# Weight comparisons spread over the last two batches with four staging slots, and the first masks made ahead of the second gates

## The chip, the cores and the metric

One Trainium2 chip, one core of it. The metric is the device time of one launch in microseconds (us). Engine names are those of the profile: PE is the matrix engine, DVE the vector engine, ACT the scalar engine, POOL the GpSimd engine, SP the engine whose queue issues most of the transfers. PEld is the weight load of PE. The kernel is written with one instruction stream for each engine and explicit semaphores, so each engine works strictly through its own list.

## The reference

One transformer-like layer on x of 16 x 256 x 256 in fp32, with a context of the same shape. First an mLSTM attention with 8 heads of 32, then a feed-forward network with ternary weights:

```
x = x + mlstm(layernorm(x), ctx, ctx, gates)      # gates: 16 columns, tanh cap, log-sigmoid, cumulative sum and max
z = layernorm(x)
h = silu(z @ w1.T * s1) * (z @ w2.T * s2)          # 256 -> 1024
h = gelu(h @ h1.T * s3)                            # 1024 -> 1024
h = gelu(h @ h2.T * s4)                            # 1024 -> 1024
x = x + h @ w3.T * s_w3                            # 1024 -> 256
```

The decay matrix of the attention is exp(log_d - row maximum) below the diagonal, multiplied on the scores of each head.

## The kernel before, in words

The 16 sequences are worked in 8 pairs (`PAIRS`), each 512 tokens wide. All weights of the feed-forward network stay in SBUF as `wgt`, 22 units (`UNITS`) of 128 x 1024 fp32, loaded once in a rounding format (fp32r). Activations are split into a high and a low part (`h_hi`, `h_lo`) in that format, and every product is done twice, once for each part, so that the result is as good as fp32 as long as the weights are exactly representable. That is tested at run time: each weight unit is loaded a second time without rounding (`load_raw`, 512 KB) and compared on DVE with the resident one (`compare`, L868). The marks of difference are counted (`inexact`), summed over columns (`decide`, L874), summed over partitions by a matmul on PE (`count_inexact`, L1176), and turned into an integer `general` (L876). At its end every engine reads `general` and branches (`if_general`): if any weight was changed by rounding, the whole feed-forward network is done again by a slow exact path. With the ternary weights of this input it never is.

The main loop runs over i = 0..7. `batch(i)` on each engine does the feed-forward network of pair i and, woven into it by hand, the attention of pair i+1 (`a_stage`) and the gates of pair i+2 (`g_stage`). So iteration 6 has no gates any more, and iteration 7 has neither. On PE an iteration is: `swiglu` (64 matmuls of 512 columns, L1105 and L1106), `hidden` for two layers (2 x 128 matmuls of 512 columns, L1129 and L1130; for the first two of the eight output tiles the sum runs as the inputs come in, and from the third on everything must be there), `project` (64 matmuls of 256 columns, L1162 and L1163). ACT makes silu or gelu and `h_hi`, DVE makes `h_lo` (L840, L844), and PE needs both.

The comparisons stand in iteration 7 on DVE: after each `lo(i, 0, m)` of the first hidden layer two of them (0 to 15), after the first three `lo(i, 1, m)` of the second another two each (16 to 21), then `decide`. The raw units go through two slots, placed in `decay`, the tile of the decay matrices, with bf16 marks beside each slot. `load_raw(n)` is issued by SP when comparison n-2 is done. SP starts these loads in iteration 7, after the store of pair 6.

Before the loop stands a prologue, which does the attention of pair 0 and the gates of pairs 0 and 1 with nothing beside them, in this order. On PE: `turn_z(0)`, `gates(0)`, some clock-keeping matmuls, `turn_z(1)`, `turn_rows(0)` (L1032, which gives the columns `cols` for the masks), `gates(1)` (L1017 with the keys and the high part, L1024 with z, which needs the low part of z from POOL, L435), `scores(0, 0)` and `scores(0, 1)` (L1050), `make_state(0)` (L1059), values and state. On DVE: scans of pair 0 (L706, L718), normalization of z of pair 1, `gain_b` (L947), `add_gate_low(1)` (L699, waits for `gates(1)`), `masks(0)` (L735, 32 operations with two SBUF inputs, `decay` and `future`, and a column of `cols`), `floors(0)` (L743), `weigh_scores(0, 0)` and `(0, 1)` (L751, four operations each, one input from PSUM). On ACT the exponentials of the masks (`decays`, L531) and the high parts, on POOL the low parts (L431, L435) and `weigh_keys` (L426). `scores(0, 1)` waits for all of `weigh_scores(0, 0)`, since both use the same PSUM banks, and `make_state(0)` for all of `weigh_scores(0, 1)`.

Of the kernel before, what the change touches and what calls it, by code (L numbers as in the profile page):

```python
# [12 lines left out]
BF16 = mybir.dt.bfloat16  # L13
# [8 lines left out]
KH = HID // P  # L22
# [9 lines left out]
PAIRS = BATCH // W  # L32
# [14 lines left out]
LAYERS = 4  # L47
GELU = 4
STAGE = 4

ROW_G, ROW_FLOOR, ROW_CHUNK = 0, 32, 64
ROWS = ROW_CHUNK + BH
# [1 line left out]
ROW_LOW = 64  # L54
SPLIT_COLS = ROW_LOW + GATE_COLS
SPLIT_WIDTH = SPLIT_COLS + HEADS

RSQRT_STEPS = 11
NORM_STEPS = 3 + RSQRT_STEPS
# [9 lines left out]
def build(nc, x, ctx_tok, ctx_t, gate_w, gate_b, outnorm_w, w_cols, scales, w3_s, out):  # L69
    with ExitStack() as stack:  # L70
# [3 lines left out]
        def sem(name):  # L74
            return stack.enter_context(nc.semaphore(name))
# [70 lines left out]
        s_raw = [sem(f"s_raw{n}") for n in range(2)]  # L146
# [134 lines left out]
        block = stack.enter_context(nc.Block())  # L281

        def raw(n):
            return decay[:, n % 2 * 3 * UNIT // 2:n % 2 * 3 * UNIT // 2 + UNIT]

        def marks(n):
            return decay[:, n % 2 * 3 * UNIT // 2 + UNIT:(n % 2 + 1) * 3 * UNIT // 2].bitcast(BF16)

        @block.sync
        def _(sp):  # L290
# [43 lines left out]
                sp.dma_start(out[i], xs[i % 2][:]).then_inc(s_out, 16)  # L334

            def load_raw(n):
                if n < 2:
                    sp.wait_ge(s_mix, MIX_STEPS * PAIRS)
                else:
                    sp.wait_ge(s_inexact, n - 1)  # L340
                sp.dma_start(raw(n), w_cols[:, n * UNIT:(n + 1) * UNIT]).then_inc(s_raw[n % 2], 16)

            load_z(0)
            sp.dma_start(gw_in, gate_w).then_inc(s_gw, 16)
# [17 lines left out]
            for i in range(PAIRS):  # L362
                j, g = i + 1, i + 2
                if j < PAIRS and j > 1:
                    load_x(j)
                if g < PAIRS:
                    load_z(g)
                    load_ctxT(g)
                    load_v(g)
                if j < PAIRS:  # L370
                    keep_x1(j)
                if g < PAIRS:
                    keep_rows(g)
                    spread_max(g)
                if i == PAIRS - 1:
                    for n in range(UNITS):
                        load_raw(n)
                store(i)
            sp.wait_ge(s_x1kept, 16 * PAIRS)
# [97 lines left out]
        def _(act):  # L477
# [120 lines left out]
            take_gate_low(0)  # L598
            soft_cap(0)
            softplus(0)  # L600
            split_keys(1)
            take_zT(1)
            take_gate_low(1)
            take_cols(0)
            soft_cap(1)
            decay_cols(0)
            decays(0)
            softplus(1)
            take_near(0)
            take_cols(1)  # L610
# [12 lines left out]
        def _(dve):  # L623
# [247 lines left out]
            def decide():  # L871

                dve.wait_ge(s_inexact, UNITS)
                dve.tensor_reduce(inexact_sum[:], inexact[:], AX.X, ALU.add).then_inc(s_inexact_sum, 1)  # L874
                dve.wait_ge(s_inexact_all, 1)
                dve.tensor_scalar(general[:], ps_a[0:1, 0, 0:1], 0.0, None, ALU.is_gt).then_inc(s_general, 1)  # L876

            def batch(i, a_stage, g_stage, last=False):
                j, g = i + 1, i + 2
                for m in range(KH):  # L880
                    swiglu(i, m)
                    if m >= 1:
                        lo_1(i, m - 1)
                lo_1(i, KH - 1)
                if a_stage:
                    masks(j)
                    floors(j)
                    weigh_scores(j, 0)
                for m in range(KH):
                    lo(i, 0, m)  # L890
                    if a_stage and m == 1:
                        weigh_scores(j, 1)
                    if g_stage and m == 3:
                        norm_1_stats(g)
                    if g_stage and m == 4:
                        norm_rsqrt(s_norm1, g)
                        norm_1_apply(g)
                    if a_stage and m == 5:
                        take_state(j)
                    if a_stage and m == 6:  # L900
                        take_far(j)
                    if a_stage and m == 7:
                        take_num(j)
                        mix_divide(j)
                    if last:
                        compare(2 * m)
                        compare(2 * m + 1)
                if a_stage:
                    mix_square(j)
                    mix_rsqrt(j)  # L910
                    residual(j)
                    norm_2_stats(j, xs[j % 2])
                for m in range(KH):
                    lo(i, 1, m)
                    if a_stage and m == 1:
                        norm_rsqrt(s_norm2, j)
                        norm_2_apply(j, xs[j % 2])
                    if g_stage and m == 2:
                        add_gate_low(g)
# [4 lines left out]
                    if last and m < 3:  # L924
                        compare(2 * KH + 2 * m)
                        compare(2 * KH + 2 * m + 1)
                    if last and m == 3:
                        decide()
                if a_stage:
                    take_z2T(j)  # L930
                finish(i)

            dve.memset(rows[:], 0.0).then_inc(s_cleared, 1)
            norm_1_stats(0)
# [13 lines left out]
            add_gate_low(1)  # L948
            dve.wait_ge(s_ident, 8)
            masks(0)  # L950
            floors(0)
            weigh_scores(0, 0)
            weigh_scores(0, 1)
            take_state(0)
            scan_f(1)
# [27 lines left out]
        def _(pe):  # L983
# [194 lines left out]
            def batch(i, a_stage, g_stage, as_is=False, last=False):  # L1178
                j, g = i + 1, i + 2
                if as_is:  # L1180
                    pe.wait_ge(s_y, W * i)
                weights_in(pe, 0)
                pe.wait_ge(s_z2lo, i + 1)
                for m in range(KH):
                    swiglu(i, m, as_is)
                    if a_stage and m == 4:
                        scores(j, 0)

                def after_2(m):
                    if a_stage and m == 3:  # L1190
                        scores(j, 1)
                    if a_stage and m == 5:
                        make_state(j)
                        values(j, 0, 0)
                    if a_stage and m == 6:
                        read_state(j)

                def after_3(m):
                    if g_stage and m == 2:
                        gates(g)  # L1200
                    if a_stage and m == 6:
                        turn_z2(j)
                    if g_stage and m == 7:
                        turn_rows(g)
                    if last and m == 5:
                        count_inexact()
# [24 lines left out]
                project(i, as_is)  # L1231

            def keep_clock(products):

# [6 lines left out]
            gates(0)  # L1241
            keep_clock(12)
            pe.wait_ge(s_cleared, 1)
            turn_z(1)
            turn_rows(0)
            gates(1)
            scores(0, 0)
            scores(0, 1)
            make_state(0)
            for b in range(W):  # L1250
# [65 lines left out]
```

## Time and profile before

| | us |
|---|---|
| median of 3 runs | 873.95 |
| lowest, highest | 872.20, 879.17 |
| profiled execution, its own time | 878.02 |
| its span, first to last instruction | 876.3 |
| mean granted TensorE clock | 0.944 of full speed |
| PE busy (matmul) | 811.6 (93%) |
| DVE busy | 564.1 (64%) |
| ACT busy | 380.3 (43%) |
| POOL busy | 62.8 (7%) |

The profiled execution took 1.7 us more than its span, and 4.1 us more than the median of the runs. A busy share of 93% on PE is an average over a prologue of about 100 us, seven iterations and a last one, and says nothing about any one of them.

### The profile page before, as it was taken

What the parts mean: (1) busy time and instruction counts of PE and PEld (TensorE: products, weight loads), DVE (VectorE), ACT (ScalarE), POOL (GpSimd) and SP (SyncE); (2) the same over time, 40 slices, a digit from 0 to 9 for tenths busy, and PEclk for the clock granted to TensorE, in tenths of its full rate; (3) what the DMA queues carried; (4) which work ended last, traced back from release to release, by engine and by line L of the source; (5) the groups of instructions that cost most, each with busy time, mean ns of one, the idle gap of its engine ahead of it and who ended that gap; (6) DMA issues with size and microseconds to landing.
All of it is one profiled execution on the core that took longest, in us unless ns stands there. A gap on an engine that the chain in (4) does not pass through costs nothing.

```text
span 876.3 us, 11793 instructions
## 1 busy us (share of the span) xinstructions
PE 811.6 (93%) x4610; PEld 692.5 (79%) x4610; DVE 564.1 (64%) x1336; ACT 380.3 (43%) x551; POOL 62.8 (7%) x54
## 2 busy tenths in 40 slices
PE   5448699999999999999999999999999999999586
PEld 5348588887888888888888888888888788888466
DVE  4474586857857585958776695758585765564551
ACT  2230363455535472355535462556345553443131
POOL 4240000200020000100020001000020000000000
PEclk7556799999999999999999999999999999999788
DMA  7573200122000400131003200040012100024650
GB/s 248 212 283 119 117 1 25 50 97 73 25 26 31 162 25 5 46 124 46 25 25 120 74 25 26 25 169 1 25 50 98 49 1 1 25 73 140 179 161 26
DMA packets 14635, 66.40 MB, mean 76 GB/s; under 512 B 2032, under 2 KB 2416, under 8 KB 11504
## 3 DMA queue, kind: packets, MB, share of 16 engines
q1 hardware_dynamic: 13280, 54.07, 17.7%
q0 software_dynamic: 1296, 11.53, 3.5%
q8 instruction: 38, 0.62, 0.3%
q14 instruction: 21, 0.17, 0.1%
HBM read 57.08 MB, written 8.52 MB: 75 GB/s over the span
## 4 chain that ended last, share of the span: by engine, by line
PE 73%; DVE 16%; DMA 5%; issue 3%; ACT 2%; POOL 1%; DVEq 0%; POOLq 0%; ACTq 0%
PE ps_f L1129 19%; PE ps_f L1130 18%; DVE decay L735 8%; PE ps_a L1068 7%; PE ps_f L1105 7%; PE ps_f L1106 7%; DMA decay<-w_cols 5%; PE ps_f L1162 4%; PE ps_f L1163 4%; DVE decay L751 2%; PE ps_a L1050 2%; PE ps_a L987 2%; DVE decay L868 2%; PE ps_a L1059 1%; PE ps_a L1078 1%
## 5 line engine op out<-in xcount | busy, mean ns | idle before, releaser
L1129 PE MATMUL ps_f<-h_hi,wgt 128*128 128x512 f32 x1024 | 407.5, 398 | 9.2 <-DVE h_lo L844 9.2
L1130 PE MATMUL ps_f<-h_lo,wgt 128*128 128x512 f32 x1024 | 401.9, 392 | 0.0
L1129 PEld LDWEIGHTS ps_f<-h_hi,wgt 128*128 128x128 f32 x1024 | 194.0, 189 | 51.5 <-DVE h_lo L844 10.7
L1130 PEld LDWEIGHTS ps_f<-h_lo,wgt 128*128 128x128 f32 x1024 | 194.1, 190 | 38.5
L844 DVE TENSOR_TENSOR h_lo<-work,h_hi 128x512 fp32r<-128x512 f32 x128 | 86.1, 688 | 125.4 <-ACT h_hi L563 124.3
L558 ACT ACTIVATE work<-ps_f,scl 128x512 f32<-128x512 f32 x128 | 87.4, 683 | 179.9 <-PE ps_f L1130 179.8
L1105 PE MATMUL ps_f<-h_hi,wgt 128*128 128x512 f32 x256 | 101.4, 396 | 0.0
L1106 PE MATMUL ps_f<-h_lo,wgt 128*128 128x512 f32 x256 | 100.3, 392 | 0.0
L545 ACT ACTIVATE work<-ps_f,scl 128x512 f32<-128x512 f32 x64 | 44.1, 689 | 92.6 <-PE ps_f L1106 92.6
L563 ACT ACTIVATE h_hi<-work 128x512 fp32r<-128x512 f32 x128 | 80.9, 632 | 4.1
L835 DVE SCALAR_TENSOR_TENSOR work<-ps_f,scl,work 128x512 f32<-128x512 f32 x64 | 48.1, 751 | 49.2 <-ACT work L545 49.2
L735 DVE SCALAR_TENSOR_TENSOR decay<-decay,cols,future 128x128 f32<-128x128 f32 x256 | 73.0, 362 | 0.0
L1068 PEld LDWEIGHTS ps_a<-v_aug,decay 128*128 128x128 f32 x512 | 67.7, 209 | 1.6
L1068 PE MATMUL ps_a<-v_aug,decay 128*128 128x33 f32 x512 | 66.0, 287 | 0.0
L1162 PE MATMUL ps_f<-wgt,h_hi 128*128 128x256 f32 x256 | 62.2, 285 | 0.0
L1163 PE MATMUL ps_f<-wgt,h_lo 128*128 128x256 f32 x256 | 61.8, 283 | 0.0
L1105 PEld LDWEIGHTS ps_f<-h_hi,wgt 128*128 128x128 f32 x256 | 48.0, 188 | 14.9 <-DVE work L835 4.0
L1106 PEld LDWEIGHTS ps_f<-h_lo,wgt 128*128 128x128 f32 x256 | 48.1, 188 | 8.7
L531 ACT ACTIVATE decay<-decay 128x1024 f32<-128x1024 f32 x32 | 33.9, 1060 | 38.7 <-DVE decay L735 38.7
L1163 PEld LDWEIGHTS ps_f<-wgt,h_lo 128*128 128x128 f32 x256 | 49.1, 192 | 0.1
L1162 PEld LDWEIGHTS ps_f<-wgt,h_hi 128*128 128x128 f32 x256 | 49.1, 192 | 0.1
L426 POOL TENSOR_TENSOR num<-v_aug,e_cols 128x256 f32<-128x256 f32 x16 | 17.3, 1099 | 377.7 <-ACT e_cols L524 377.7
(148 smaller groups left out, 785.7 us busy)
## 6 DMA issues: line engine op xcount, KB each, us to landing
decay<-m_rows SPq DMA_DIRECT2D x16, 1024.0 KB, 5.9
decay<-w_cols SPq DMA_DIRECT2D x22, 512.0 KB, 4.2
wgt<-w_cols POOLq DMA_DIRECT2D x5, 1024.0 KB, 9.5
v_aug<-ctx_tok SPq DMA_DIRECT2D x8, 528.0 KB, 3.7
z<-x SPq DMA_DIRECT2D x8, 512.0 KB, 4.4
xs<-x SPq DMA_DIRECT2D x8, 512.0 KB, 3.6
wgt<-w_cols POOLq DMA_DIRECT2D x2, 2048.0 KB, 9.8
x_kept<-xs SPq DMA_DIRECT2D x8, 512.0 KB, 2.6
```

The costliest lines, as they stand in the source:

```text
L558: act.activation(work[:, m % GELU], ps_f[:, (turn_of(i) + m) % 4], ACT.Gelu, scale=scl[:, 2 + layer, m:m + 1]).then_inc(s_gelu, 1)
L563: act.activation(h_hi[1 - layer][:, m], work[:, m % GELU], ACT.Copy).then_inc(s_hi, 1)
L735: last = dve.scalar_tensor_tensor(part, part, cols[:, t, row:row + 1], future[:], ALU.subtract, ALU.add)
L835: dve.scalar_tensor_tensor(work[:, 2 + m % 2], ps_f[:, bank], scl[:, 1, m:m + 1], work[:, m % 2], ALU.mult, ALU.mult).then_inc(s_hf, 1)
L844: dve.tensor_tensor(h_lo[1 - layer][:, m], work[:, m % GELU], h_hi[1 - layer][:, m].bitcast(F32), ALU.subtract).then_inc(s_lo, 1)
L1068: last = pe.matmul(ps_a[:, 2 + b, h * DV:(h + 1) * DV], decay_of(b, h, t), v_aug[:, b * TILES + t, h, :], start=True, stop=True)
L1105: pe.matmul(ps_f[:, bank + half], w, moving(z2_hi[:, c], as_is), start=(c == 0), stop=False)
L1106: last = pe.matmul(ps_f[:, bank + half], w, moving(z2_lo[:, c], as_is), start=False, stop=(c == CH - 1))
L1129: pe.matmul(ps_f[:, bank], w, moving(h_hi[layer][:, k], as_is), start=(k == 0), stop=False)
L1130: last = pe.matmul(ps_f[:, bank], w, moving(h_lo[layer][:, k], as_is), start=False, stop=(k == KH - 1))
L1162: pe.matmul(to, moving(h_hi[0][:, k, q * P:(q + 1) * P], as_is), w, start=(k == 0), stop=False)
L1163: last = pe.matmul(to, moving(h_lo[0][:, k, q * P:(q + 1) * P], as_is), w, start=False, stop=(k == KH - 1))
```

## The change

Two parts. (1) The comparisons are spread over iterations 6 and 7. The raw units get four slots of their own, which fill `decay`; the marks move to `z`, which nothing reads after pair 7 is normalized. Comparisons 0 to 5 stand in iteration 6, one after each `lo(6, 1, m)` for m = 2 to 7; 6 to 13 in the first and 14 to 21 in the second hidden layer of iteration 7, one after each `lo`. SP issues loads 0 to 9 in iteration 6, before the store of pair 6, and the others after it. The sum over columns is taken before `finish(7)`, the matmul of the count stands after the last `project`, and `general` is made after `finish(7)`. (2) In the prologue PE turns the rows of pair 0 before z of pair 1, and does `scores(0, 0)` before `gates(1)`. ACT takes the columns of pair 0 before the keys of pair 1, and its exponentials stand ahead of the low gates of pair 1. DVE makes the masks, the floors and the first weighted scores of pair 0 before `add_gate_low(1)`.

```
 def raw(n):
-    return decay[:, n % 2 * 3 * UNIT // 2:n % 2 * 3 * UNIT // 2 + UNIT]
+    return decay[:, n % RAW * UNIT:(n % RAW + 1) * UNIT]          # RAW = 4
 def marks(n):
-    return decay[:, ... ].bitcast(BF16)
+    return z[:].rearrange("p q d -> p (q d)")[:, n % 2 * UNIT // 2:(n % 2 + 1) * UNIT // 2].bitcast(BF16)

 SP  load_raw(n)
-    if n < 2:   sp.wait_ge(s_mix, MIX_STEPS * PAIRS)
-    else:       sp.wait_ge(s_inexact, n - 1)
+    if n < RAW: sp.wait_ge(s_mix, MIX_STEPS * PAIRS)
+    else:       sp.wait_ge(s_inexact, n - RAW + 1)
 SP  loop over i, after keep_x1, keep_rows, spread_max
+    if i == PAIRS - 2:
+        for n in range(COMPARED_BEFORE_LAST + RAW): load_raw(n)    # COMPARED_BEFORE_LAST = 6
     if i == PAIRS - 1:
-        for n in range(UNITS): load_raw(n)
+        for n in range(COMPARED_BEFORE_LAST + RAW, UNITS): load_raw(n)

 DVE compare(n)
-    dve.wait_ge(s_raw[n % 2], 16 * (n // 2) + 16)
+    dve.wait_ge(s_raw[n % RAW], 16 * (n // RAW) + 16)
+    if n >= 2:
+        dve.wait_ge(s_inexact, n - 1)
 DVE batch, first hidden layer, after lo(i, 0, m)
     if last:
-        compare(2 * m); compare(2 * m + 1)
+        compare(COMPARED_BEFORE_LAST + m)
 DVE batch, second hidden layer, after lo(i, 1, m)
-    if last and m < 3: compare(2 * KH + 2 * m); compare(2 * KH + 2 * m + 1)
-    if last and m == 3: decide()
+    if last: compare(COMPARED_BEFORE_LAST + KH + m)
+    elif a_stage and not g_stage and m >= KH - COMPARED_BEFORE_LAST:
+        compare(m - KH + COMPARED_BEFORE_LAST)
 DVE batch, end
+    if last: sum_inexact()          # the reduction that stood in decide()
     if a_stage: take_z2T(j)
     finish(i)
+    if last: decide()               # waits for the count, makes general
 PE  batch
-    if last and m == 5: count_inexact()      # in the second hidden layer
     project(i, as_is)
+    if last: count_inexact()

 ACT prologue                 DVE prologue                   PE prologue
  softplus(0)                  gain_b += 1                    wait s_cleared
 +take_cols(0)                -add_gate_low(1)               +turn_rows(0)
 +decay_cols(0)                wait s_ident                   turn_z(1)
  split_keys(1)                masks(0)                      -turn_rows(0)
  take_zT(1)                   floors(0)                     +scores(0, 0)
 +decays(0)                    weigh_scores(0, 0)             gates(1)
  take_gate_low(1)            +add_gate_low(1)               -scores(0, 0)
 -take_cols(0)                 weigh_scores(0, 1)             scores(0, 1)
  soft_cap(1)
 -decay_cols(0)
 -decays(0)
  softplus(1)
```

## Rows read from the trace of the kernel before

**Rows 1.** The page, granted TensorE clock in tenths, 40 equal slices.

```profile
PEclk7556799999999999999999999999999999999788
```

**Rows 2.** Waits of PE, 756 to 876.3 us: total, times, longest.

```profile
PE ps_f L1129 <- DVE h_lo L844: 9.2, 3, 4.3
PE ps_a L1176 <- DVE inexact_sum L874: 3.3, 1, 3.3
```

**Rows 3.** Chain that ended last, 725 us to the end: start, length, what.

```profile
...
794.04 1.24 DVE decay L868 x2
795.30 3.73 DMA decay<-w_cols
...
```

**Rows 4.** Timeline of PE, 756 us to the end: start, length, instruction.

```profile
...
762.60 0.28 PE L1162 MATMUL ps_f<-wgt,h_hi 128*128 128x256 f32 x1
...
770.27 0.40 PE L1105 MATMUL ps_f<-h_hi,wgt 128*128 128x512 f32 x1
...
785.00 0.39 PE L1129 MATMUL ps_f<-h_hi,wgt 128*128 128x512 f32 x1
...
794.12 0.39 PE L1129 MATMUL ps_f<-h_hi,wgt 128*128 128x512 f32 x1
...
869.11 0.28 PE L1163 MATMUL ps_f<-wgt,h_lo 128*128 128x256 f32 x1
```

**Rows 5.** Two-microsecond stretch: busy of PE, PEld, DVE, ACT, POOL; clock; DMA.

```profile
826.00:828.00 2.00, 1.82 (x4) 0.90 (x4) 1.23 (x2) 0.00 (x0) 0.00 (x0) 0.50 0.82 242
```

**Rows 6.** Timeline of DVE and SP in iterations 6 and 7.

```profile
745.05 0.34 SPq L330 DMA_DIRECT2D x_kept<-xs  x1
...
751.91 1.90 DVE L844 TENSOR_TENSOR h_lo<-work,h_hi 128x512 fp32r<-128x512 f32 x3
...
765.10 1.22 DVE L826 TENSOR_TENSOR h_lo<-ps_a,h_hi 128x1024 fp32r<-128x1024 f32 x1 [0.22 <-ACT h_hi L540]
...
794.04 1.22 DVE L868 SCALAR_TENSOR_TENSOR decay<-decay,wgt 128x1024 bf16<-128x1024 f32 x1
```

**Rows 7.** All transfers into `decay` by SP, from issue to landing.

```profile
DMA to landing us min/median/max: 3.4/4.6/7.4
```

**Rows 8.** Timeline of SP, the last instruction of the list.

```profile
871.34 0.34 SPq L334 DMA_DIRECT2D out<-xs  x1
```

**Rows 9.** Timeline of the prologue and the start of iteration 0.

```profile
25.28 2.33 POOL L431 TENSOR_TENSOR h_lo<-ctxT,h_hi 128x1024 fp32r<-128x1024 f32 x1 [5.74 <-ACT h_hi L484]
25.45 2.71 DVE L718 TENSOR_TENSOR_SCAN state<-rows 16x256 f32<-16x256 f32 x1
...
34.79 0.29 DVE L947 TENSOR_SCALAR gain_b<-gain_b 128x256 f32<-128x256 f32 x1
...
38.90 2.35 POOL L435 TENSOR_TENSOR h_lo<-zT,h_hi 128x1024 fp32r<-128x1024 f32 x1 [11.28 <-ACT h_hi L493]
...
44.20 8.49 DVE L735 SCALAR_TENSOR_TENSOR decay<-decay,cols,future 128x128 f32<-128x128 f32 x32
...
46.24 7.51 POOL L426 TENSOR_TENSOR num<-v_aug,e_cols 128x256 f32<-128x256 f32 x2 [3.95 <-ACT e_cols L524]
...
53.19 2.47 DVE L751 SCALAR_TENSOR_TENSOR decay<-ps_a,decay 128x512 f32<-128x512 f32 x4
...
55.71 2.09 PE L1050 MATMUL ps_a<-work 32*128 32x128 f32 x32 [9.38 <-DVE decay L751]
...
60.50 2.10 PE L1059 MATMUL ps_a<-v_aug,num 128*128 128x132 f32 x8 [2.70 <-DVE decay L751]
...
64.41 0.68 DVE L718 TENSOR_TENSOR_SCAN xs<-rows 16x256 f32<-16x256 f32 x1
...
118.63 9.21 DVE L735 SCALAR_TENSOR_TENSOR decay<-decay,cols,future 128x128 f32<-128x128 f32 x32
...
119.73 1.39 POOL L426 TENSOR_TENSOR num<-v_aug,e_cols 128x256 f32<-128x256 f32 x2 [64.38 <-ACT e_cols L524]
```

**Rows 10.** Chain that ended last, 20 to 60 us.

```profile
41.30 2.06 PE ps_f L1024 x8
```

More of the change, by code:

```diff
@@ L49 @@
 STAGE = 4
+RAW = 4
 ROW_G, ROW_FLOOR, ROW_CHUNK = 0, 32, 64
@@ L56 @@
 SPLIT_WIDTH = SPLIT_COLS + HEADS
+COMPARED_BEFORE_LAST = 6
 RSQRT_STEPS = 11
@@ L145, in build @@
         s_wgt = [sem(f"s_wgt{n}") for n in range(LAYERS)]
-        s_raw = [sem(f"s_raw{n}") for n in range(2)]
+        s_raw = [sem(f"s_raw{n}") for n in range(RAW)]
         s_inexact = sem("s_inexact")
@@ L283, in raw @@
         def raw(n):
-            return decay[:, n % 2 * 3 * UNIT // 2:n % 2 * 3 * UNIT // 2 + UNIT]
+            return decay[:, n % RAW * UNIT:(n % RAW + 1) * UNIT]
         def marks(n):
-            return decay[:, n % 2 * 3 * UNIT // 2 + UNIT:(n % 2 + 1) * 3 * UNIT // 2].bitcast(BF16)
+            return z[:].rearrange("p q d -> p (q d)")[:, n % 2 * UNIT // 2:(n % 2 + 1) * UNIT // 2].bitcast(BF16)
         @block.sync
@@ L336, in load_raw @@
             def load_raw(n):
-                if n < 2:
+                if n < RAW:
                     sp.wait_ge(s_mix, MIX_STEPS * PAIRS)
                 else:
-                    sp.wait_ge(s_inexact, n - 1)
-                sp.dma_start(raw(n), w_cols[:, n * UNIT:(n + 1) * UNIT]).then_inc(s_raw[n % 2], 16)
+                    sp.wait_ge(s_inexact, n - RAW + 1)
+                sp.dma_start(raw(n), w_cols[:, n * UNIT:(n + 1) * UNIT]).then_inc(s_raw[n % RAW], 16)
             load_z(0)
@@ L374, in _ @@
                     spread_max(g)
+                if i == PAIRS - 2:
+                    for n in range(COMPARED_BEFORE_LAST + RAW):
+                        load_raw(n)
                 if i == PAIRS - 1:
-                    for n in range(UNITS):
+                    for n in range(COMPARED_BEFORE_LAST + RAW, UNITS):
                         load_raw(n)
@@ L600, in _ @@
             softplus(0)
+            take_cols(0)
+            decay_cols(0)
             split_keys(1)
             take_zT(1)
+            decays(0)
             take_gate_low(1)
-            take_cols(0)
             soft_cap(1)
-            decay_cols(0)
-            decays(0)
             softplus(1)
@@ L866, in compare, with sum_inexact, decide @@
                         weights_in(dve, layer)
-                dve.wait_ge(s_raw[n % 2], 16 * (n // 2) + 16)
+                dve.wait_ge(s_raw[n % RAW], 16 * (n // RAW) + 16)
+                if n >= 2:
+                    dve.wait_ge(s_inexact, n - 1)
                 dve.scalar_tensor_tensor(marks(n), raw(n), 1.0, wgt[:, n * UNIT:(n + 1) * UNIT].bitcast(F32),
                                          ALU.mult, ALU.not_equal, accum_out=inexact[:, n:n + 1]).then_inc(s_inexact, 1)
-            def decide():
+            def sum_inexact():
                 dve.wait_ge(s_inexact, UNITS)
                 dve.tensor_reduce(inexact_sum[:], inexact[:], AX.X, ALU.add).then_inc(s_inexact_sum, 1)
+            def decide():
                 dve.wait_ge(s_inexact_all, 1)
@@ L905, in batch @@
                     if last:
-                        compare(2 * m)
-                        compare(2 * m + 1)
+                        compare(COMPARED_BEFORE_LAST + m)
                 if a_stage:
@@ L923, in batch @@
                         scan_m(g)
[L924 to L928, printed above, removed]
+                    if last:
+                        compare(COMPARED_BEFORE_LAST + KH + m)
+                    elif a_stage and not g_stage and m >= KH - COMPARED_BEFORE_LAST:
+                        compare(m - KH + COMPARED_BEFORE_LAST)
+                if last:
+                    sum_inexact()
                 if a_stage:
@@ L931, in batch @@
                 finish(i)
+                if last:
+                    decide()
             dve.memset(rows[:], 0.0).then_inc(s_cleared, 1)
@@ L947, in _ @@
             dve.tensor_scalar(gain_b[:], gain_b[:], 1.0, None, ALU.add).then_inc(s_gain, 1)
-            add_gate_low(1)
             dve.wait_ge(s_ident, 8)
@@ L952, in _ @@
             weigh_scores(0, 0)
+            add_gate_low(1)
             weigh_scores(0, 1)
@@ L1204, in after_3 @@
                         turn_rows(g)
-                    if last and m == 5:
-                        count_inexact()
                 def within_2(m):
@@ L1231, in batch @@
                 project(i, as_is)
+                if last:
+                    count_inexact()
             def keep_clock(products):
@@ L1243, in _ @@
             pe.wait_ge(s_cleared, 1)
+            turn_rows(0)
             turn_z(1)
-            turn_rows(0)
+            scores(0, 0)
             gates(1)
-            scores(0, 0)
             scores(0, 1)
```

## The prediction

> **What bounds the kernel now.** I read the granted clock first [rows 1]. It is full for most of the run and low at both ends, in the prologue and again in the last three slices, from about 810 us. A low clock at the end means that PE had been standing still. The waits of PE in that stretch [rows 2] name who: three waits for a low part from DVE, 9.2 us, and one for the sum of the marks, 3.3 us. They are 12.5 us in all, and between the start of iteration 7 and those waits there is no other. The chain of work that ended last [rows 3] says what DVE was doing: two comparisons, then a load of raw weights, and that pattern repeats 11 times. With two slots and two comparisons in a row DVE always catches up with the loads, and `lo` stands behind them in its queue. So iteration 7 is bound by the loads. Iterations 0 to 6 are bound by PE, which has no gap there. The prologue is bound by a chain over several engines, with PE mostly waiting.
>
> **Part 1, the last iteration: what PE would need.** All terms are from one timeline [rows 4]. `swiglu` runs from 770.27 to 785.00, 14.73 us. The hidden layers run at one matmul in 0.228 us where nothing waits: 40 matmuls lie between the starts at 785.00 and 794.12. 256 of them are 58.4 us. `project` of iteration 6 lasts from 762.60 to 770.27, 7.67 us. Sum: 80.8 us, so the last product would end at 851.0. Before, the last one starts at 869.11 and ends about 0.12 later, at 869.2. The difference is 18.2 us, of which 12.5 are the waits [rows 2]; the other 5.7 are products at half clock after each wait [rows 5], 0.43 instead of 0.23 us each, and refilling.
>
> Does the new placing hold those 18.2? In iteration 7 one comparison of 1.22 us [rows 6] follows each `lo` of 0.69. PE needs one output tile of 16 matmuls, 3.65 us, for each `lo`, so DVE has 1.7 us to spare each time. Only the first two tiles of a layer come as a pair, and nothing is needed of them before the next layer. The last `lo` of a layer is the tight one: PE asks for it after 28 matmuls of the next layer, 6.4 us on (in `project` after 28 of 0.12, 3.4 us). It takes 0.7 (gelu), 0.6 (high part) and 0.7 us, and the comparison before it ended long ago. No wait there.
>
> The loads: a slot is free after its comparison and needed again four comparisons later, 4 x 3.65 - 1.2 = 13.4 us. Loads into `decay` took 3.4 to 7.4 us [rows 7]. The margin is 6 us at the worst measured landing. Only at the start, with four in flight after the copy of x1, are they slower than a pair was, bounded below by 3.4 and above by four times the median, 18 us. I take about 10 us for the fourth, nearest to two in flight at 3.7 us of bare waiting [rows 3].
>
> **Iteration 6.** SP issues the first four right after the copy of x1 at 745.05 [rows 6], so from about 745.4 to 746.8. The first comparison stands after the third `lo`. Before, three `lo` ran together at 751.91, because DVE was busy with the normalization until then, so comparison 0 starts at about 752.6, 7 us after its load was issued. Six comparisons, 7.3 us, now go between 752.6 and the last `lo` at about 764.2; DVE was idle for over 9 us of that stretch. The last comparison moves `take_z2T(7)` from 765.10 [rows 6] to about 766.1, done at 767.4, and PE asks for it at 770.27 [rows 4]. What is queued behind a late load here: `lo(6, 1, m)`, then that, then `finish(6)`, whose bank PE wants again in `swiglu`. The cover is about 3 us, and costs one for one beyond it. SP holds the store of pair 6 behind loads 0 to 9; the last of these waits for comparison 5 at about 766, and the store was due at 772. The marks in `z` cost nothing, and neither does the added wait on comparison n-2, which is older work of the same engine. Cost of iteration 6: 0, up to 2.
>
> **The end.** The count's matmul stands after the last product, and `general` after `finish(7)`, so all engines take their branch about 2 us after the last product and no earlier. The store, issued at 871.34 with the span's end 5.0 us later [rows 8], covers it: SP must wait for its landing anyway. I take 0.2 us; bounds 0 and 2, since no row shows a branch by itself. Part 1: -18.2 + 0.2 = -18.0 us.
>
> **Part 2, the prologue.** Before, the masks start at 44.20, after `gates(1)` and `add_gate_low(1)` [rows 9]. What they need is there earlier: DVE is free after L947, at 35.08, the rows have been scanned since 29 us and their broadcast was issued at 29.6, so landed by 37.0 at the latest by its 7.4 [rows 7]; turning the rows and taking the columns is 1 us and fits before. So the masks start at 35.1 (or up to 37), last 8.5, and with the floors the first weighted scores start at 44.3 in place of 53.19: 8.9 us less. After that the order is as before: 2.5 us of weighing, `scores(0, 1)` 2.1 us, weighing again, then `make_state(0)` at 51.6 in place of 60.50. On ACT the exponentials (1.06 us each) come after the high part of z at about 38.8, when two masks are finished or nearly so; they keep up. On PE `scores(0, 0)`, 2.1 us, now stands before `gates(1)`, but the second half of `gates(1)` waits until POOL is done at 41.25 anyway.
>
> That half waits for POOL's low part of z, 38.90 to 41.25 [rows 9], and now this subtraction meets the masks, which it did not before. Three places in rows 9 show what such a meeting costs. A scan of 0.68 us (at 64.41) took 2.71 when POOL's L431 ran (at 25.45): DVE was held for the whole of POOL's operation. The first weighing of keys, which takes 1.39 at 119.73, took 7.51 at 46.24, until the masks ended: POOL was held. And at 118.63 the masks took 9.21 instead of 8.49: both shared. If DVE is held, the masks grow by 2.35 and the gain is 8.9 - 2.35 = 6.6. If POOL is held until the masks end at 43.6, its subtraction ends at about 46, the second half of `gates(1)` (2.06 [rows 10]) at 48.1 and `scores(0, 1)` behind it in PE's queue starts at 48.1 in place of 46.9: gain 7.7. `add_gate_low(1)` in DVE's queue then waits until about 48.9, still before `scores(0, 1)` is done. If nothing is held, 8.9. I take 7.2, between the first two, since all three rows show a price.
>
> The Trainium skill (GPSIMD Engine Reference, section 8, Key points) says that GpSimd shares its SBUF interfaces with VectorE and contends with instructions that have two SBUF inputs. The masks have two, the weighing has one, so by that rule the meeting costs in the masks alone; the three rows agree that it costs, and only they say how much. Without that rule the sum would be 1.7 us lower.
>
> The moved L431 is neutral: it held the scan at 25.45 for 2.0 us, and after the change it falls on the small steps of the normalization of pair 1 instead, which are held as long. L947 ends where it did, within 0.5 us.
>
> Everything behind `make_state(0)` is relative to it: the values at half clock, the clock-keeping products, the mixing. The clock may change its levels at another point of that sequence. In slices 3 and 4 [rows 1] it stays near half while PE does the small products of the attention, so I expect no rise there; the phase is worth 1.5 us either way.
>
> **Sum.** 878.02 (the profiled execution's own time) - 18.0 - 7.2 = 852.8. The median of the runs is 4.1 lower. If those 4.1 lie in the stretch bound by loads, they go with it, and all runs come to about 852.8; if they lie elsewhere, the median comes to 848.7. The loads are what varies most in this trace (3.4 to 7.4 us for the same kind), so I lean to the first: 851.5.
>
> **Rivals.**
> - The tail keeps a part. If four loads in flight land late or DVE's queue makes PE wait in spite of my slack, some waits of [rows 2] stay, each with its stretch at half clock; half of 18.2 is 9.1, so about 861. For it: six new comparisons in the busiest stretch of DVE. Against: 13.4 us for a load of at most 7.4. Chance 0.08.
> - The prologue gives nothing. Something between 60 and 100 us may be set by the clock or by a transfer, not by `make_state(0)`, or both holdings above add up. 878.02 - 18.0 = 860, or 857 with half the gain. Against: the chain runs through L1059 and on without a transfer. Chance 0.09.
> - More than the sum: no holding at all, and the clock rises during the denser products at 35 to 43 us and stays for part of the attention. 845. Chance 0.06.
> - Slower: the loads are slower than the comparisons ask. If a load took 20 us with four in flight, a round of four comparisons would take 21.3 us in place of 14.6, and the 5.5 rounds cost 37 us: 890. It eats the whole gain from about 18 us a load, and starts to cost at 13.4. The slowest of all in the trace is 7.4 [rows 7]. Chance 0.02.
> - It doesn't do what it says: the waits of PE simply move from one iteration to the other, near 872. Against: iteration 6 has over 9 us of idle DVE. Chance 0.02.
>
> **How the numbers follow.** The forecast has 0.73. A measurement of this kernel can tell about 1%, 8.7 us, from no change; everything under 865.2 is faster by that. Forecast, partial tail, empty prologue and the better case lie there: 0.96. Same: 0.02. Slower: 0.02. The range goes from the better case, 845, to the empty prologue, 860, and leaves out less than 2 in 10.
>
> **What would show it.** In the new profile: no wait of L1129 for L844 from iteration 6 on, clock 1.0 to the end, six L868 between about 735 and 760 and 16 later, none of them right behind another but at the start of a layer; last product about 81 us after the first L1105 of iteration 7; `make_state` (L1059's line) at 51 to 54 us; a POOL subtraction longer than 2.35 us or masks longer than 8.5. It is wrong if PE waits at the start of the last `project` or `swiglu`, if comparisons in iteration 6 show idle time for a load longer than 3 us, or if the span's end lies more than 6 us behind the last store.

## The result, and the profile after

Median 851.49 us (850.59 to 853.00) against 874.37; ratio 0.9727, 95% interval 0.9699 to 0.9755 (the two medians alone give 0.9738). The profiled execution took 851.26, its span is 849.5: 26.8 us less than before in one pair of profiles.

The page of the changed kernel, its granted clock and the chain that ended last by engine (PE was 73% and the transfers 5% of it before):

```profile
PEclk7756899999999999999999999999999999999999
PE 80%; DVE 16%; ACT 2%; issue 2%; DMA 0%; POOL 0%; DVEq 0%; ACTq 0%
```

The low digits at the end [rows 1] are gone; those of the prologue are still there. The busy time in iteration 7, by one stretch (busy of PE, PEld, DVE, ACT, POOL; clock; DMA share; GB/s):

```profile
761.00:842.00 81.00, 81.00 (x391) 67.81 (x389) 42.85 (x69) 32.01 (x49) 0.00 (x0) 1.00 0.29 85
```

PE is busy for 81.00 of 81.00 us, at clock 1.00. The list of PE's waits has nothing in it from 100 us to the end; both rows of [rows 2] are gone. The timeline, PE with the last product, DVE and SP at the end:

```profile
761.63 0.40 PE L1116 MATMUL ps_f<-h_hi,wgt 128*128 128x512 f32 x1
...
841.99 0.28 PE L1174 MATMUL ps_f<-wgt,h_lo 128*128 128x256 f32 x1
...
844.11 0.14 DVE L885 TENSOR_SCALAR general<-ps_a 1x1 int32<-1x1 f32 x1
844.22 0.34 SPq L337 DMA_DIRECT2D out<-xs  x1
```

From the first product of iteration 7 to the end of its last one it is 842.11 - 761.63 = 80.48 us (the last product is counted with 0.12 us, its distance from the one before); before it was 869.23 - 770.27 = 98.96 [rows 4]. That is 18.48 us less. From there to the span's end it is 7.39 in place of 7.07.

DVE in iteration 6, around the first and the last comparison of the six (compare [rows 6]):

```profile
743.27 0.69 DVE L850 TENSOR_TENSOR h_lo<-work,h_hi 128x512 fp32r<-128x512 f32 x1
743.88 1.22 DVE L876 SCALAR_TENSOR_TENSOR z<-decay,wgt 128x1024 bf16<-128x1024 f32 x1
...
756.15 1.22 DVE L876 SCALAR_TENSOR_TENSOR z<-decay,wgt 128x1024 bf16<-128x1024 f32 x1
757.29 0.08 DVE L876 DVE_READ_ACCUMULATOR z<-decay,wgt 128x1 f32 x1
757.29 1.22 DVE L832 TENSOR_TENSOR h_lo<-ps_a,h_hi 128x1024 fp32r<-128x1024 f32 x1
```

No idle time stands before a comparison, in either iteration: no load was late. L832, `take_z2T(7)`, ends at 758.5, 3.1 us before PE asks for it.

The prologue (compare [rows 9]):

```profile
23.43 0.68 DVE L724 TENSOR_TENSOR_SCAN state<-rows 16x256 f32<-16x256 f32 x1
...
27.29 2.33 POOL L437 TENSOR_TENSOR h_lo<-ctxT,h_hi 128x1024 fp32r<-128x1024 f32 x1 [9.76 <-ACT h_hi L490]
27.35 2.30 DVE L642 TENSOR_SCALAR nw<-nw 128x4 int32<-128x4 int32 x1
...
33.08 8.48 DVE L741 SCALAR_TENSOR_TENSOR decay<-decay,cols,future 128x128 f32<-128x128 f32 x32
...
36.91 6.86 POOL L441 TENSOR_TENSOR h_lo<-zT,h_hi 128x1024 fp32r<-128x1024 f32 x1 [7.29 <-ACT h_hi L499]
...
41.48 2.40 DVE L749 TENSOR_SCALAR floor<-e_cols 128x16 f32<-128x16 f32 x2
...
43.80 2.47 DVE L757 SCALAR_TENSOR_TENSOR decay<-ps_a,decay 128x512 f32<-128x512 f32 x4
...
51.12 2.10 PE L1070 MATMUL ps_a<-v_aug,num 128*128 128x132 f32 x8 [2.70 <-DVE decay L757]
```

The subtraction for the low part of z took 6.86 us in place of 2.35: POOL was held until the masks ended at 41.56. Then DVE was held in turn: the two floors took 2.40 us in place of 0.6. The state of pair 0 starts 27.69 us after the scan of pair 0 starts (51.12 - 23.43); before it was 60.50 - 25.45 = 35.05. That is 7.36 us less.

But the scan itself starts 2.02 us earlier, and nothing of the change lies ahead of it. The kernel before has this in its timeline:

```profile
8.10 2.34 POOL L431 TENSOR_TENSOR h_lo<-work,h_hi 128x1024 fp32r<-128x1024 f32 x1 [3.32 <-ACT h_hi L484]
8.27 2.19 DVE L639 SCALAR_TENSOR_TENSOR nw<-nw 128x4 f32<-128x4 f32 x1
```

A step of 0.16 us in the normalization of pair 0 took 2.19, since POOL began its subtraction on the first context just then. In the profile after, the first context came 2.1 us later and POOL began at 10.19, when this chain was over. So 2.0 of the 26.8 us between the two profiles are chance: the profiles of e1, e2, e4 and e5 below have such a held step, with and without the change, and those of e3, e6 and e9 have none.

The whole account in us, before to after: start to scan -2.02; scan to state -7.36; state to the first product of iteration 0 +0.46 (39.01 to 39.47); iterations 0 to 6 +0.28 (670.76 to 671.04); iteration 7 -18.48; end +0.32. Sum -26.8.

### The profile page after: what moved, and what is told of

The parts are those of the page before. It is cut to its first block, busy times and chain, and to the rows that moved or that the text cites. A ratio compares the mean times of both kernels' runs of the same rounds, so it can differ in the third digit from the quotient of the medians.

```text
span 849.5 us, 11813 instructions
## 1 busy us (share of the span) xinstructions
PE 805.2 (95%) x4610; PEld 689.1 (81%) x4610; DVE 564.8 (66%) x1336; ACT 380.3 (45%) x551; POOL 61.0 (7%) x54
## 4 chain that ended last, share of the span: by engine, by line
PE 80%; DVE 16%; ACT 2%; issue 2%; DMA 0%; POOL 0%; DVEq 0%; ACTq 0%
PE ps_f L1140 22%; PE ps_f L1141 21%; DVE decay L741 8%; PE ps_a L1079 7%; PE ps_f L1116 7%; PE ps_f L1117 7%; PE ps_f L1173 4%; PE ps_f L1174 4%; DVE decay L757 2%; PE ps_a L1061 2%; PE ps_a L998 2%; PE ps_a L1070 1%; PE ps_a L1089 1%; PE ps_a L1035 1%; PE ps_a L1028 1%
## 5 line engine op out<-in xcount | busy, mean ns | idle before, releaser
L850 DVE TENSOR_TENSOR h_lo<-work,h_hi 128x512 fp32r<-128x512 f32 x128 | 86.5, 690 | 135.0 <-ACT h_hi L569 133.9
L1116 PEld LDWEIGHTS ps_f<-h_hi,wgt 128*128 128x128 f32 x256 | 48.2, 188 | 14.9 <-DVE work L841 4.0
L846 DVE TENSOR_TENSOR h_lo<-work,h_hi 128x512 fp32r<-128x512 f32 x64 | 43.7, 683 | 0.8
```

Of the source, the lines that this page charges most:

```text
L850: dve.tensor_tensor(h_lo[1 - layer][:, m], work[:, m % GELU], h_hi[1 - layer][:, m].bitcast(F32), ALU.subtract).then_inc(s_lo, 1)
L1116: pe.matmul(ps_f[:, bank + half], w, moving(z2_hi[:, c], as_is), start=(c == 0), stop=False)
```

## The experiments

Each is timed beside runs of the kernel before on the same chip, and ratios are to those. Twelve kernels ran.

### Is it the sum of its two parts?

e1 keeps the comparisons of the changed kernel and has the prologue's order of before. e2 is the kernel before with the prologue's new order.

```
e1: prologue of ACT, DVE and PE as in the "-" lines of the change; the rest as changed
e2: prologue of ACT, DVE and PE as in the "+" lines of the change; the rest as before
```

> The changed kernel with the prologue's order of before. If the two parts are independent and sized as I read them (tail 18.2 us, prologue 7.2 us plus what the change of clock phase does), this takes about 18 us less than before: 856 to 858 against a median of 874.4. If the prologue's part was worth nothing and the tail everything, it takes 851.5, as the changed kernel. If the tail is worth less without the prologue, it is above 860. First product of iteration 7 about 99 us before the last in before, 80.5 us here.

> The kernel before with the new order of the prologue alone. By the sum: 7 us less than before, 867 (865 to 869), iteration 7 as in before with its 12 us of waits of PE. The rival that the prologue gives nothing: 874. From the scan of pair 0 to the state of pair 0 the time falls from 35.05 to about 27.7 us, as in the changed kernel. If the spread of the runs of before (7 us) comes from the loads in the tail, the runs of this one spread as widely, and those of the tail-only kernel within 3 us.

e1: 860.23 us (858.57 to 860.66), ratio 0.9806 (0.9777 to 0.9834), which is 17.0 us (14.6 to 19.5) of the 876.6 of before. e2: 870.13 (867.00 to 871.77), ratio 0.9924 (0.9897 to 0.9950), 6.7 us (4.4 to 9.0). Together 23.7, and the change as a whole is 0.9727, 23.9 us. The parts add up, as far as intervals of 4 to 5 us can tell. Their medians lie 2 to 3 us above what I wrote, and that of the kernel before beside them lies 2.2 higher too (876.6 in place of 874.4).

Iteration 7 takes 80.5 us in e1 (770.75 to 851.23). In e2 PE's waits are there again, a little shorter than in [rows 2]:

```profile
PE ps_f L1129 <- DVE h_lo L844: 7.5, 3, 4.1
PE ps_a L1176 <- DVE inexact_sum L874: 2.7, 1, 2.7
```

There iteration 7 takes 858.56 - 762.58 = 95.98 us, 3.0 less than in the profile of before, in the fastest of e2's five runs. So the stretch bound by loads varies by some microseconds, from one profile each. The runs of e2 spread by 4.8 us and those of e1, without that stretch, by 2.1. Both are as I wrote, but the 2.1 that are left need another source; that is at e7.

### Four slots, or two iterations?

The change does both. e3 does the spreading with two slots. e4 has four slots and all 22 comparisons in iteration 7. Both keep a third thing that the change moved: the sum of the marks and its matmul, for which PE waited 3.3 us [rows 2], stand at the end.

```
e3:  RAW = 2
e4:  SP: all load_raw(n) in iteration 7
     DVE, first hidden layer of iteration 7, after lo(7, 0, m):
         m < 6:  compare(2 * m); compare(2 * m + 1)     else: compare(6 + m)
     DVE, second hidden layer: compare(14 + m) as changed; none in iteration 6
```

> The changed kernel with two slots in place of four; the comparisons stay spread over two iterations. A slot is then needed again after 2 x 3.65 - 1.2 = 6.1 us, and landings are 3.3 to 7.8 us, median 4.5. If spreading does the work and the slots are a margin: 851 to 853, PE without waits in iteration 7, DVE with a few waits for loads. If the four slots do the work: DVE waits at most comparisons, PE waits at the end of each layer, 857 or more.

> The changed kernel with all 22 comparisons in iteration 7: two after each of the first six low parts of the first hidden layer, one after every other. Four slots. The loads of a pair have 2 x 3.65 - 2.4 = 4.9 us to land after both slots are free, against a median of 4.5 for one and more for two at once. If what bounded before was two comparisons catching up with two slots, four slots give back most of the 18.2 us: 852 to 856. If one comparison for each low part is what is needed, DVE waits for loads as before and PE loses 5 us or more: 857 to 865.

e3: 851.83 (849.71 to 853.16), ratio 0.9715 (0.9683 to 0.9748). e4: 851.99 (850.48 to 853.65), ratio 0.9712 (0.9680 to 0.9745). Both are the changed kernel's time. The waits of DVE for raw weights from 700 us on, first in e3, then in e4; before they were 24.6 us in 19 waits:

```profile
DVE z L876 <- DMA decay<-w_cols: 4.6, 6, 1.6
```

```profile
DVE z L873 <- DMA decay<-w_cols: 1.2, 3, 0.6
```

PE waits for nothing in either. So spreading over two iterations does the whole of it without four slots (e3), and with four slots the comparisons need not start in iteration 6 (e4). With two slots and one comparison for each low part, DVE waits 4.6 us for loads, and none of it reaches PE. With four slots and two comparisons in a row there is 1.2 us of waiting. In e4 the time is at the good end of the 852 to 856 that I had written: DVE has 3.1 us of work (two comparisons and a low part) per 3.65 us and works off what it has lost. But e4 doesn't show that four slots alone are enough. It has only six pairs in a row and then one comparison for each low part, where the kernel before has eleven pairs. Four slots with before's placing weren't run, and neither was before with only the count moved.

### What does POOL's subtraction cost among the masks?

```
e5:  DVE: floors(0) ahead of masks(0)
e6:  DVE: floors(0); masks(0); weigh_scores(0, 0); weigh_scores(0, 1); add_gate_low(1)
     PE:  scores(0, 0); gates(1), first half; scores(0, 1); gates(1), second half; make_state(0)
```

> The changed kernel with the floors made before the masks on DVE. After the change the floors took 2.40 us in place of 0.6, while POOL worked on its held subtraction, and the first weighted scores started at 43.80. If POOL only holds instructions with two SBUF inputs or none from PSUM, the weighing starts right behind the masks, 41.6, and the state of pair 0 comes no more than 0.3 us earlier, since the scores of the second sequence stand behind the low gates in PE's queue (44.0 to 46.0): 851 to 852, no difference that can be told. If the weighing is held too, its first operation takes 2.9 us and nothing moves at all.

> Floors first, and on PE the second half of the gates of pair 1 behind the second scores of pair 0; add_gate_low(1) on DVE behind the second weighing. This takes POOL's held subtraction off the path of pair 0. If the meeting of POOL and the masks is what cost the prologue 1.7 us or more, the state of pair 0 comes at 48.7 in place of 51.1 on the clock of the changed kernel, 2.4 us: about 849. If something later (gates of pair 1, clock phase) binds, 851.5.

e5: 852.38 (850.37 to 853.06), ratio 0.9731 (0.9697 to 0.9766), no difference to the changed kernel. The weighing follows the masks at once and is not held, though POOL's subtraction runs beside it:

```profile
38.91 7.03 POOL L441 TENSOR_TENSOR h_lo<-zT,h_hi 128x1024 fp32r<-128x1024 f32 x1 [7.08 <-ACT h_hi L499]
...
43.63 2.48 DVE L757 SCALAR_TENSOR_TENSOR decay<-ps_a,decay 128x512 f32<-128x512 f32 x4
...
52.76 2.10 PE L1070 MATMUL ps_a<-v_aug,num 128*128 128x132 f32 x8 [2.70 <-DVE decay L757]
```

Yet the state comes 27.30 us after the scan (52.76 - 25.46), 0.4 less than 27.69, since `scores(0, 1)` now waits behind the gates in PE's queue. e6 takes that away as well (its masks run from 33.21 to 41.69, and POOL's subtraction beside them takes 7.02):

```profile
41.61 2.48 DVE L757 SCALAR_TENSOR_TENSOR decay<-ps_a,decay 128x512 f32<-128x512 f32 x4
...
44.15 2.09 PE L1063 MATMUL ps_a<-work 32*128 32x128 f32 x32 [6.19 <-DVE decay L757]
...
48.94 2.10 PE L1072 MATMUL ps_a<-v_aug,num 128*128 128x132 f32 x8 [0.72 <-DVE decay L757]
50.83 6.88 PE L1081 MATMUL ps_a<-v_aug,decay 128*128 128x33 f32 x32
```

48.94 - 23.41 = 25.53 us from scan to state, 2.16 less than in the changed kernel; I had written 2.4. Of that, 0.39 is the new place of the floors, which e5 has too. POOL's held subtraction on the path is the rest, 27.30 - 25.53 = 1.77. The changed kernel says the same: its masks start 9.65 us after the scan in place of 18.75, 9.10 earlier, and its state 7.36 earlier, 1.74 less. So the meeting cost 1.7 to 1.8 us there. Median 848.27, ratio 0.9675 (0.9624 to 0.9726), and in the same session 4.1 us below e5. Three of its runs lie at 848 to 850 and one at 842.6, which 2 us of order can't make. The mean granted clock of that run is 0.972, that of the others 0.959 to 0.961.

### Is the spread of one kernel's runs the meeting in the normalization of pair 0?

```
e7:  POOL: wait_ge(s_gw_split, 5) ahead of split_keys_low(0)
e8:  e6 and e7, and ACT: split_keys(1) ahead of soft_cap(0)
```

> The changed kernel, but POOL starts its first subtraction only when the gate weights are split, so that it never holds DVE in the normalization of pair 0. In the profiled runs of before and of the runs with the longer time, one step there took 2.19 us instead of 0.16 and all that follows came 2.0 us later; it depends on when the first context lands. If this is what spreads the runs of one kernel, all runs lie within 1 us at 850.6; if it isn't, they spread over 2 to 3 us as before, around 851.5. If the later start delays the first gates, 852 or more.

> The last two together, and on ACT the keys of pair 1 before the tanh of pair 0, so that POOL's subtraction for them falls into a stretch in which DVE waits, and not on the normalization of pair 1 (one step of 2.30 us there). 0.6 us are lost on ACT and 2.1 won on DVE. If the holdings are priced rightly: 850.6 - 2.4 - 1.5 = 847, runs within 1.5 us. If the phase of the clock takes it back, 849 to 850.

e7: 850.25 (849.54 to 850.85), ratio 0.9713 (0.9681 to 0.9745): a spread of 1.3 us at the lower end of the changed kernel's 850.6 to 853.0, where e5 beside it has 850.4 to 853.1. In the normalization of pair 0 one step took 2.2 us in the profiles of before, e1, e2, e4 and e5; with the wait none can be held so. Four runs within 1.3 us speak for this race as a source of the spread, but they are few, and the clock was full from 48 to 51 us in the profile of e7, so its runs aren't free of the clock either.

e8: median 838.28, runs at 837.94, 837.97, 838.58 and 846.81; ratio 0.9608 (0.9549 to 0.9667). I had written 847. The one run at 846.8 fits the sum; three are 9 us better. The timeline of one of those, PE from the second scores on:

```profile
42.01 2.09 PE L1064 MATMUL ps_a<-work 32*128 32x128 f32 x32 [6.01 <-DVE decay L758]
...
46.80 1.14 PE L1073 MATMUL ps_a<-v_aug,num 128*128 128x132 f32 x8 [1.03 <-DVE decay L758]
47.78 3.66 PE L1082 MATMUL ps_a<-v_aug,decay 128*128 128x33 f32 x32
51.27 1.15 PE L1092 MATMUL ps_a<-state,work 128*128 128x132 f32 x8
52.25 3.91 PE L1082 MATMUL ps_a<-v_aug,decay 128*128 128x33 f32 x32
```

and the same values in the changed kernel:

```profile
53.01 6.88 PE L1079 MATMUL ps_a<-v_aug,decay 128*128 128x33 f32 x32
59.70 2.11 PE L1089 MATMUL ps_a<-state,work 128*128 128x132 f32 x8
61.59 6.88 PE L1079 MATMUL ps_a<-v_aug,decay 128*128 128x33 f32 x32
```

The granted clock was at 0.5 (1.2 GHz) for all of the attention there, and at 1.0 (2.4 GHz) from 45 to 55 us in e8. From scan to state e8 takes 46.80 - 23.39 = 23.41 us, 4.28 less than the changed kernel, and from the state to the turn of the rows behind the values 9.18 in place of 17.16, 7.98 less. So the order bought 4 us, and the clock 8. The run at 846.8 is one where the clock did less: its mean granted clock is 0.964, against 0.970 to 0.976 in the others.

In e8 PE had run from 42.0 to 45.7 without a gap and then stood for 1.0 us, where it stands for 2.7 in the changed kernel. That is not what decides. In the profile of e6 PE ran from 44.15 to 48.2 without a gap and then stood for 0.72 us, and the clock stayed at 0.5 (values in 6.88 us).

### The clock ahead of the attention, by itself

```
e9:   changed kernel, PE: scores(0, 1); keep_clock(12); make_state(0)
e10:  e8, PE: gates(1), first half; keep_clock(26); scores(0, 1)
e11:  e10, PE: turn_rows(1); keep_clock(100) in place of 24
e12:  e10, PE: turn_rows(1); keep_clock(58) in place of 24
```

> The changed kernel with 12 clock-keeping products in the 2.7 us in which PE waits between the second scores and the state of pair 0, and nothing else. In the changed kernel PE ran the attention of pair 0 (53 to 68 us) at half clock, 15.3 us for products that took 8.5 us in the last run of the rounds before, where PE had had no gap ahead of them and the clock was full. If a gap just ahead of the state is what leaves the clock at half, and products of that small size keep it where it is for a while, this gains 5 to 8 us: 843 to 846. If the small products do not hold a full clock, 850 to 852. The 24 matmuls themselves cost 0 if the gap covers them, 0.5 us at most beyond.

> The combination of all the moves of the prologue, with 26 clock-keeping products in the gap of 6 us ahead of the second scores. Of the combination's four runs three came at 838 and one at 846.8, which I read as the clock missing its rise ahead of the attention. If so, the products fill the gap, all runs lie at 837 to 839 and none at 846. If the long run had another cause, one of about four stays long.

> The run beside it with 100 in place of 24 clock-keeping products behind the attention, where PE otherwise stands still for 10 us and the clock falls to half before z of the feed-forward network is turned. The turn then takes 1.0 in place of 2.0 us and the first products are at full speed: 1.0 to 1.5 us less, 836 to 837. If the clock is at half when they start, they last longer than the gap and cost up to 5 us.

> The combination with 26 clock-keeping products ahead of the second scores, and 58 products behind the attention in place of 24 (the run with 100 overfilled the gap: 24.2 us of products, 0.12 us a matmul at full clock and two matmuls a product, against a gap of 17 us). 58 products last 14.0 us at full clock, so PE stands still for 3 us instead of 11.5 before the turn of z, and the turn takes 1.04 instead of 1.97 us: 836 to 837 against 837.8. If the clock is at half when they start they last 24 us and cost 7: then runs at 843 to 845.

e9: median 846.84 (844.53 to 848.71), ratio 0.9655 (0.9628 to 0.9682): about 0.7% below the changed kernel for 24 matmuls in a gap. Its state and values:

```profile
50.98 1.07 PE L1070 MATMUL ps_a<-v_aug,num 128*128 128x132 f32 x8
51.88 3.65 PE L1079 MATMUL ps_a<-v_aug,decay 128*128 128x33 f32 x32
55.37 1.71 PE L1089 MATMUL ps_a<-state,work 128*128 128x132 f32 x8
56.87 6.88 PE L1079 MATMUL ps_a<-v_aug,decay 128*128 128x33 f32 x32
```

The first half of the values ran at full clock, then the clock fell (at about 56 us), with PE busy all the time, and the second half took its 6.88 us. From the state to the turn of the rows behind the values it is 12.6 us against 17.2. So this is the clock's doing and not the order's, and the answer lies between the two that I had set out.

e10: 837.80 (836.98 to 843.74), ratio 0.9565 (0.9533 to 0.9596). Five of six runs are within 1.2 us, the sixth is at 843.7. In the profile of e8 the clock is full from 35 to 38.4 us, falls, and rises again at 45; with the gap filled it stays full from 36 to 63. But that didn't remove the long run. No profile shows that run; its mean granted clock is 0.971, against 0.975 to 0.979 in the others.

e11: 849.06 (841.37 to 849.74), ratio 0.9666 (0.9630 to 0.9702). e12: 837.53 (837.00 to 842.26), ratio 0.9611 (0.9568 to 0.9655). The products behind the attention in e11, then in e12 with the turn of z behind them, then the turn in e10:

```profile
54.94 24.17 PE L1250 MATMUL ps_f<-ident 128*128 128x128 f32 x200
```

```profile
55.14 14.78 PE L1250 MATMUL ps_f<-ident 128*128 128x128 f32 x116
72.22 1.42 PE L999 MATMUL ps_a<-ident,num 128*128 128x128 f32 x8 [2.30 <-DVE num L668]
```

```profile
72.63 1.97 PE L999 MATMUL ps_a<-ident,num 128*128 128x128 f32 x8 [11.51 <-DVE num L668]
```

e11 was my mistake of counting: a clock-keeping product is two matmuls of 0.12 us at full clock, so 100 last 24 us and push everything behind them. In the profile the first product of iteration 0 starts at 82.57 in place of 77.29 in e10, 5.3 us later. The profiled run is one of the two short ones (842.81, clock 0.985). The other four are at 849 with clock 0.977 to 0.978, so the half clock costs them some 6 us more. e12 fits the gap, and turns z 0.5 us faster, with nothing left of it in the median. Two of its six runs are at 841 to 842, again with the lower mean clock (0.975 and 0.978, against 0.981 to 0.983). The best version is e10 or e12, which can't be told apart: medians of 837.8 and 837.5, on different chips, and by the ratios 1.2 to 1.7% below the changed kernel.

## Why the prediction was right

**The bound.** Right. The waits of DVE for loads fell from 24.6 us to nothing, PE's two rows of waits went with them, and the last iteration became 80.48 us; my sum from the 0.228 us product was 80.8.

**18.2 us in the last iteration.** 18.48 between the profiles, 17.0 (14.6 to 19.5) by e1. The split in 12.5 of waits and the rest at half clock stands: clock 0.91 and 86.5 us busy of 99.0 in the same stretch before, 1.00 and all of it after. What I had not seen is that the change does more than is needed: e3 has the whole gain with two slots, e4 without a comparison in iteration 6. The margin I worked out, 13.4 us against 7.4, was far more than needed. No transfer into `decay` took more than 7.8 us to land in the new profile, so the 10 us that I took for the fourth of four loads was too much.

**Iteration 6 at no cost.** Right: +0.28 us for iterations 0 to 6, no idle time before a comparison. The first comparison started 7.1 us after its load was issued at 736.78, as worked out (7), behind the third `lo`. The cover of `take_z2T(7)` was 3.1 us where I had 3.

**The end, +0.2.** It was 0.32.

**Masks at 35.1, 8.9 us earlier, less the meeting.** The total was right, 7.36 against 7.2 (e2: 6.7, 4.4 to 9.0). Its mechanism was half right. I gave two cases, POOL held or DVE held, with the gates in PE's queue as the price of the first. Both happened one after the other: POOL was held for 4.5 us until the masks ended, then DVE for 1.8 us in the floors, and the late weighing set the time of `scores(0, 1)`, 0.45 us behind the gates. The price was 1.7 to 1.8 us (e5 and e6) where I had 1.7, so it was sized right from bounds on either side and not from the course that it took. The rule of the Trainium skill (GPSIMD Engine Reference, section 8, Key points: contention with instructions in a two-port mode or with two SBUF inputs) agrees with what e5 shows: the masks met POOL and it took 7.03 us, the weighing, with one input in PSUM, ran beside it in its usual 2.48. But the floors and L642 have one SBUF input each and were held too (2.40 and 2.30 us). My reading of the rule, that the meeting costs in the masks alone, left out its other half, the two-port mode; no run shows in which mode they ran.

**The moved L431 as neutral.** Right: it left the scan (2.71 to 0.68 us) and took a step of the normalization instead (L642, 2.30). 

**The clock's phase, 1.5 us either way.** For the change as made it was right, +0.46 us. As a bound on what the clock can do there it was wrong: I took the half clock in the attention as given, because the clock digits were near half. The profiles of e9 and e8 show 4.6 and 8.0 us in it, and one run of e6 at 842.6 shows that it can come by chance. My rival of the better case, 845, had the right mechanism and too small a price.

**Which time to subtract from.** I leaned to the loads as the source of the 4.1 us between the profiled execution and the median. 2.0 of it was the meeting in the normalization of pair 0, which the change doesn't touch; the profiles of e4 and e5 still have it. The loads account for some of the rest: iteration 7 took 96.0 us in one profile and 99.0 in another. My two parts came to 25.2 us and the measured ratio makes them 23.9; the lean took 2.8 off, so that 851.5 was a fall of 22.4 from the median of before, and the medians fell by 22.9. The parts were 1.3 us too large and the lean covered that, so 851.5 to the tenth was met by luck.

## What to carry to other kernels

When an engine stalls on loads, look at both sides before doing both: how many transfers are in flight and how much work is asked for in a row; here spreading the work with two slots removed all of the stall, and so did four slots with half of the pairs left. A sum of a stretch without waits, from the spacing of its own products, gave the new length within 0.4 us, and the price of a stall is that stall and the slow products behind it. In a prologue, ask of each operation on POOL which work on DVE it will meet, in both directions, and read the clock beside every row on PE: the full clock in the attention was worth 8.0 us (e8), more than the 7.4 that the change's new order gave, and 24 matmuls in a gap alone gave 4.6 (e9).

## What the runs showed of the hardware that was not expected

- POOL and DVE hold each other by turns. A subtraction of 2.35 us on POOL took 6.9 to 7.0 us beside 32 masks on DVE with no gap between them, and ended 2.2 us after the last mask. A DVE step of 0.16 us took 2.2 to 2.3 us when it came right behind the start of POOL's, also when it was a multiply and add on 128 x 4 integers with one input in SBUF (L642), and the floors, one input each, took 2.40. Which of the two is held isn't settled: the weighing of keys on POOL took 7.51 us among the masks of the prologue and 1.39 among those of iteration 0, where the masks grew by 0.7 [rows 9].
- That meeting sits on a race with the landing of the first context: the scan starts 2 us later when POOL meets the normalization (25.4 to 25.6 us in five profiles, against 22.6 to 23.8 in the others). With a single wait against it (e7) four runs spread by 1.3 us, where those of the changed kernel spread by 2.4 and those of e5 by 2.7.
- The granted clock fell from 1.0 to 0.5 in the middle of the values of pair 0 in e9, with PE busy by the profile all the while, and stayed full through the same products in e10. Which of the two happens differs between versions and, by the times and mean clocks of e6, e8, e10, e11 and e12, between runs of one version: in each of these the longer runs have the lower mean clock. Why was not settled.
